# A fused attention and expert kernel on one core: the last stage moved into the main block, the expert tables made in three steps

## What is computed

```python
x = L0_attn_x                                   # 8 batches x 512 tokens x 256
x = x + _layernorm(_L0_attn_ref(_layernorm(x), ...))
x = x + _layernorm(_L0_ffn_ref(_layernorm(x), w_router, w1, b1, w2, b2))
# _L0_attn_ref: token attention with 16 heads, then channel attention with 8 heads
# _L0_ffn_ref, 8 experts, hidden width 1024, two experts per token:
probs = softmax(xf @ w_router); topk_w, topk_idx = top_k(probs, 2)
weights = sum(topk_w[..., None] * one_hot(topk_idx), axis=1)
h = gelu(einsum('te,ieh->tih', xf, w1) + b1)
out = sum((einsum('tih,ihe->tie', h, w2) + b2) * weights[..., None], axis=1)
```

## Time and profile before

| | us |
|---|---|
| runs of before, median (lowest to highest of 3) | 1127.04 (1125.57 to 1129.49) |
| the profiled execution | 1118.23 |
| its span, first to last instruction | 1116.4 |
| TensorE busy | 1032.4 (92%) |
| VectorE busy | 671.4 (60%) |
| ScalarE busy | 721.1 (65%) |
| GpSimd busy | 384.5 (34%) |
| mean granted TensorE clock | 0.975 |

### The profile page before, as it was taken

How to read it: one execution, slowest core, us unless ns; L and a number is a source line. 1 busy time by engine, 2 the same in 40 slices (tenths; PEclk the granted TensorE clock), 3 DMA queues, 4 the chain that set the end, 5 groups by cost and what they waited for, 6 DMA issues and landing times. The chain is left out here.

```text
span 1116.4 us, 17406 instructions
## 1 busy us (share of the span) xinstructions
PE 1032.4 (92%) x5756; PEld 702.8 (63%) x5756; DVE 671.4 (60%) x1902; ACT 721.1 (65%) x1106; POOL 384.5 (34%) x353
## 2 busy tenths in 40 slices
PE   5899999999999999998899996999999999989966
PEld 3234545555455455544588875888888888878842
DVE  5225265454735645354785777677677776679927
ACT  2797767667776766666655662676677766768804
POOL 5121030513323141224426243444433443254315
PEclk9899999999999999999999987999999999989989
DMA  7673816427082542832433133334443344446456
GB/s 267 133 246 61 264 31 204 122 84 256 18 261 73 174 150 69 275 148 91 147 100 115 62 135 123 124 133 148 147 161 119 138 143 142 151 143 224 149 215 256
DMA packets 48960, 167.47 MB, mean 150 GB/s; under 512 B 10160, under 2 KB 16688, under 8 KB 42864
## 3 DMA queue, kind: packets, MB, share of 16 engines
q1 hardware_dynamic: 38170, 136.94, 36.9%
q0 software_dynamic: 10560, 29.14, 8.2%
q10 hardware_dynamic: 150, 0.41, 0.2%
HBM read 102.74 MB, written 63.70 MB: 149 GB/s over the span
## 5 line engine op out<-in xcount | busy, mean ns | idle before, releaser
L589 ACT ACTIVATE E<-PS,VV 128x1024 f32<-128x1024 f32 x256 | 271.6, 1119 | 73.7 <-PE PS L974 72.6
L1737 PE MATMUL PH<-XP,W1P 128*128 128x512 f32 (+1 forms) x1104 | 233.1, 369 | 4.9 <-DVE HP L1678 4.5
L1737 PEld LDWEIGHTS PH<-XP,W1P 128*128 128x128 f32 x1104 | 185.8, 192 | 44.5 <-DVE HP L1678 8.1
L974 PE MATMUL PS<-OPB,OPA 102*128 102x512 bf16 x512 | 137.9, 386 | 11.4 <-DMA OPB<-norm_parts 5.7
L1678 DVE TENSOR_TENSOR HP<-PH,HP 128x512 fp32r<-128x512 f32 x156 | 106.7, 686 | 64.8 <-ACT HP L1584 64.3
L957 PE MATMUL PO<-E,VA 128*32 128x512 f32 x1024 | 143.5, 610 | 0.0
L1579 ACT ACTIVATE PH<-PH,B 128x512 f32<-128x512 f32 (+1 forms) x184 | 107.5, 596 | 53.9 <-PE PH L1737 44.9
L1502 POOL DMA_INDIRECT choice_rows<-Y,DI x78 | 79.3, 1016 | 182.3 <-DVE Y L1635 160.8
L974 PEld LDWEIGHTS PS<-OPB,OPA 102*128 102x128 bf16 x512 | 37.7, 98 | 155.4 <-ACT E L589 68.7
L1570 ACT CAST W2P<-WG 128x512 fp32r<-128x512 f32 x92 | 56.9, 621 | 103.6 <-PE PB L1768 63.6
L462 POOL DMA_INDIRECT expert_rows<-PAY,SLOT x64 | 62.7, 979 | 157.5 <-issue 80.1
(11 more groups left out here) (254 smaller groups left out, 1611.2 us busy)
## 6 DMA issues: line engine op xcount, KB each, us to landing
expert_rows<-ZERO SPq DMA_DIRECT2D x8, 4160.0 KB, 12.8
WG<-experts SPq DMA_DIRECT2D x23, 1152.0 KB, 5.1
WG<-experts SPq DMA_DIRECT2D x23, 1028.0 KB, 5.2
OPB<-q_parts SPq DMA_DIRECT2D x192, 64.0 KB
YC<-choice_rows SPq DMA_DIRECT2D x8, 1024.0 KB, 13.0
q_parts<-QP SPq DMA_DIRECT2D x48, 128.0 KB
OPA<-q_parts SPq DMA_DIRECT2D x31, 192.0 KB
X<-x SPq DMA_DIRECT2D x8, 512.0 KB, 11.1
```

Source lines behind the costliest of these rows:

```text
L589: a.activation(E[:, s % 2, h, :, :], PS[:, u % 2, :, :], ACT.Exp, scale=vec("tau_t")[:, 4 * (s // 2) + h:4 * (s // 2) + h + 1]).then_inc(e ...
L974: ins = t.matmul(PS[:, u % 2, jc, :], OPA[0:KA, m, key:key + P], OPB[0:KA, m, hh * N:hh * N + N], start=True, stop=True)
L1737: last = m.matmul(PH[:, u % BANKS, at:at + w], W1P[:, a, k * HID + c * P:k * HID + c * P + P], XP[:, o, k, 0:w], start=(k == 0 and (a, o) ...
```

## The change

The tables are made in three steps. `fill_begun` runs a second time, for the pairs 5 and 6 that the counts of batches 0 to 6 fix, in four sections at slots 18 to 21; BEGUN becomes 7, so units 5 and 6 are no longer joined. `fill_tables` makes the rest (25 subtiles where it were 29) in nine sections at slots 73 to 81. Both are generators that yield between sections. The steps of batch 7 behind `x2t` stand further apart. GpSimd gathers every unit at its usual place. The last stage's instructions follow the units' in the same block; SP waits for the last sends itself; the 16 warm-up matmuls are gone. Its work is cut into ten pieces: TensorE sums eight, GpSimd two (3 and 6, a batch each), roots are taken in six groups, GpSimd adds X for five pieces and VectorE for five; the sums of the last batch go to PB.

```diff
-BEGUN = -(-(2 * N * (B - 2) - NE * (2 * SUB - 1)) // (2 * SUB))
+KNOWN = [-(-(2 * N * b - NE * (2 * SUB - 1)) // (2 * SUB)) for b in (B - 2, B - 1)]
+BEGUN = KNOWN[-1]
...
-           17: [('prefix', B - 2)], 18: [('x2t', B - 1)], 20: [('qkc', B - 1)], 22: [('gram', B - 1)], 24: [('dist', B - 1)],
-           25: [('soft_c', B - 1)], 27: [('weights_c', B - 1)], 29: [('mix', B - 1)], 31: [('weff', B - 1)], 33: [('chan', B - 1)],
-           36: [('chan_add', B - 1)], 37: [('chan_stats', B - 1)], 39: [('chan_norm', B - 1)], 42: [('z3t0', B - 1)],
-           43: [('z3t1', B - 1)], 44: [('logits', B - 1)], 45: [('soft', B - 1)], 46: [('top', B - 1)], 50: [('prefix', B - 1)],
-           52: [('tables', B - 1)]}
+           17: [('prefix', B - 2)], 18: [('begin', B - 2), ('x2t', B - 1)], 19: [('begin', B - 2)], 20: [('begin', B - 2)], 21: [('begin', B - 2)], 22: [('qkc', B - 1)], 25: [('gram', B - 1)],
+           28: [('dist', B - 1)], 30: [('soft_c', B - 1)], 33: [('weights_c', B - 1)], 36: [('mix', B - 1)], 39: [('weff', B - 1)],
+           42: [('chan', B - 1)], 46: [('chan_add', B - 1)], 49: [('chan_stats', B - 1)], 53: [('chan_norm', B - 1)],
+           57: [('z3t0', B - 1)], 59: [('z3t1', B - 1)], 61: [('logits', B - 1)], 63: [('soft', B - 1)], 65: [('top', B - 1)],
+           71: [('prefix', B - 1)], **{k: [('tables', B - 1)] for k in range(73, 82)}}
...
+            known = [fill_begun(nc, dve, table_links, begun_ready, COUNT, const, QR[:, :, :].rearrange("p k n -> p (k n)"), TAKEN, tables, 0),
+                     fill_begun(nc, dve, table_links, begun_ready, COUNT, const, OT[:, :, :].rearrange("p g n -> p (g n)"), TAKEN, tables, 1)]
+            others = fill_tables(nc, dve, table_links, tables_ready, COUNT, TAKEN, const,
+                                 OT[:, :, :].rearrange("p g n -> p (g n)"), tables)
             def begin(b, par):
                 if isinstance(b, int) and b == B - 3:
-                    fill_begun(nc, dve, table_links, begun_ready, COUNT, const, QR[:, :, :].rearrange("p k n -> p (k n)"), TAKEN, tables)
+                    for _ in known[0]:
+                        pass
+                if isinstance(b, int) and b == B - 2:
+                    next(known[1], None)
             do["begin"] = begin
 
             def rest(b, par):
-                fill_tables(nc, dve, table_links, tables_ready, COUNT, TAKEN, const,
-                            OT[:, :, :].rearrange("p g n -> p (g n)"), tables)
+                next(others, None)
             do["tables"] = rest
             return do
 
...
-            experts = stage2(nc, make(apart), tables, tables_ready, const, rows, ys, experts1, experts2, begun, PB)
+            inner = ExitStack()
+            y_sent, y_rows, experts = stage2(nc, make(inner), tables, tables_ready, const, rows, ys, experts1, experts2, begun, PB)
+            inner.close()
+            last = stage3(nc, make(apart), X, const, HALF[:, :, :].rearrange("p a c -> p (a c)"), PB, ys, out, y_sent, y_rows)
             block = apart.enter_context(nc.Block())
...
             @block.vector
             def _(dve):
...
                 units()
+                last.vector(dve)
...
-        stage3(nc, make, X, const, ys, out)
...
     rows_of, most = COUNT[:, 0, :], STEPS_E // 2 - 1
...
     link(v.reduce_sum(full, over, AX.X))
+    if stage:
+        link(v.tensor_tensor(full, full, TAKEN[:, :], ALU.subtract))
+        link(v.tensor_tensor(ahead[:, 0:NE - 1], TAKEN[:, 1:NE], TAKEN[:, 0:NE - 1], ALU.subtract))
+        link(v.memset(ahead[:, NE - 1:NE], 0.0))
+        link(v.tensor_tensor(ahead, full, ahead, ALU.subtract))
+    yield
...
     for i in range(3):
+        yield
         link(v.tensor_tensor(picked, held, steps[:, i, :].unsqueeze(1).to_broadcast([P, S, VE]), ALU.mult))
         link(v.reduce_sum(chosen[:, i, :], picked, AX.X))
...
         for t in range(NUNITS):
+            if t == KNOWN[0]:
+                sp.wait_ge(begun["begun_ready"], 2)
...
-                        if t + 2 < NUNITS and t + 2 != BEGUN:
+                        if t + 2 < NUNITS:
                             gather_rows(t + 2)
                     at_slot(k)
-                    if k == REST_AT:
-                        gather_rows(BEGUN)
                 for c in range(HC):
                     k = first_slot(t) + groups_of(t) + c
                     if c == HC - 2 and t + 1 < NUNITS:
                         weigh_bias(t + 1)
                     at_slot(k)
-                    if k == REST_AT:
-                        gather_rows(BEGUN)
             send(NUNITS - 1)
-            for r in range(2):
-                pool.wait_ge(y_sent[r], 16 * turn_blocks(NUNITS - 1 - (NUNITS - 1 - r) % 2))
         return units
...
+    PIECES = [(0, 0, 2), (0, 2, 2)] + [(b, 0, C) for b in range(1, B - 1)] + [(B - 1, 0, 2), (B - 1, 2, 2)]
+    BY_PE, BY_POOL = (0, 1, 2, 4, 5, 7, 8, 9), (3, 6)
+    ROOTS = [(0, 1), (2,), (3, 4), (5,), (6, 7), (8, 9)]
+    POOL_ADDS = (0, 1, 2, 3, 6)
+    STORE_ORDER = (0, 1, 2, 4, 5, 3, 7, 6, 8, 9)
...
+    def total(i):
+        b, c, n = PIECES[i]
+        if i in BY_POOL:
+            return YC[:, b, 0, c:c + n, :]
+        if b == B - 1:
+            return PB[:, c // 2, :].rearrange("p (c e) -> p c e", c=2)
+        return S[:, BY_PE.index(i) % SLOTS, 0:n, :]
...
+    def sync(sp):
+        for r in range(2):
+            sp.wait_ge(y_sent[r], y_rows[r])
+        for i, (b, c, n) in enumerate(PIECES):
+            sp.dma_start(YC[:, b, :, c:c + n, :], yv[b][:, :, c:c + n, :]).then_inc(loaded[i], 16)
+        for i in STORE_ORDER:
+            b, c, n = PIECES[i]
+            sp.wait_ge(added[i], 1)
+            sp.dma_start(ov[b][:, c:c + n, :], T[:, b, c:c + n, :]).then_inc(stored, 16)
...
+    def tensor(pe):
+        m = nc.tensor
+        for at, i in enumerate(BY_PE):
+            b, c, n = PIECES[i]
+            pe.wait_ge(loaded[i], 16)
+            if at >= SLOTS and b < B - 1:
+                pe.wait_ge(normed, rows_before(BY_PE[at - SLOTS] + 1))
+            for a in range(0, n, 2):
+                for k in range(2):
+                    last = m.matmul(total(i)[:, a:a + 2, :].rearrange("p c e -> p (c e)"), const("ident"),
+                                    YC[:, b, k, c + a:c + a + 2, :].rearrange("p c e -> p (c e)"), start=(k == 0), stop=(k == 1))
+            last.then_inc(summed[i], 1)
...
+        def add_up(i):
+            b, c, n = PIECES[i]
+            pool.wait_ge(loaded[i], 16)
+            g.tensor_tensor(YC[:, b, 0, c:c + n, :], YC[:, b, 0, c:c + n, :], YC[:, b, 1, c:c + n, :], ALU.add).then_inc(summed[i], 1)
+        def root(k):
+            at = columns(ROOTS[k][0], ROOTS[k][-1])
+            pool.wait_ge(var_ready, 2 * (k + 1))
+            g.tensor_tensor(R[:, 2, at], R[:, 0, at], half[:, 0:at.stop - at.start], ALU.pow).then_inc(roots, 1)
+            pool.wait_ge(roots, k + 1)
+            g.tensor_tensor(R[:, 3, at], R[:, 1, at], R[:, 2, at], ALU.mult).then_inc(scaled, 1)
+        root(0)
+        add_up(3)
+        add(0)
+        root(1)
+        add(1)
+        add_up(6)
+        root(2)
+        add(2)
+        root(3)
+        root(4)
+        add(3)
+        root(5)
+        add(6)
...
+        for k, group in enumerate(ROOTS):
+            for i in group:
+                b, c, n = PIECES[i]
+                dve.wait_ge(summed[i], 1)
+                for a in range(n):
+                    link(v.bn_stats(ST[:, columns(i).start + a, :], total(i)[:, a, :]))
+            dve.wait_ge(links, at[0])
+            cols = columns(group[0], group[-1])
+            for a in range(cols.start, cols.stop):
+                link(v.bn_aggr(MV[:, a, :], ST[:, a, :]))
+            dve.wait_ge(links, at[0])
+            v.tensor_scalar_add(R[:, 0, cols], MV[:, cols, 1], EPS).then_inc(var_ready, 1)
+            v.tensor_scalar_mul(R[:, 1, cols], MV[:, cols, 0], -1.0).then_inc(var_ready, 1)
+            if k >= LAG:
+                for i in ROOTS[k - LAG]:
+                    if i not in POOL_ADDS:
+                        add(i)
+        for k in range(len(ROOTS) - LAG, len(ROOTS)):
+            for i in ROOTS[k]:
+                if i not in POOL_ADDS:
+                    add(i)
```

197 lines of the change are left out of this document (88 added, 109 removed).

## The result

| | before | changed | ratio |
|---|---|---|---|
| first comparison, median us (lowest to highest) | 1126.3 (1123.9 to 1129.5) | 1138.3 (1135.4 to 1140.3) | 1.0094 [1.0058, 1.0130] |
| the same kernel once more, below | 1119.5 | 1118.6 | 0.9982 [0.9958, 1.0007] |
| profiled execution (span) | 1118.2 (1116.4) | 1137.5 (1135.7) | |

Slower by 0.94%, where 0.7% faster was forecast (1119.5 against 1127.0). A comparison is a set of kernels measured side by side with the kernel before. Both rows of ratios are needed: what the change costs depends on pauses of TensorE that come in some comparisons and not in others, and the profile of before that I read was taken without them.

The account below looks back on a forecast made before the run. TensorE was taken as the bound, VectorE close behind. Tail -1.6 and last stage -6.0 gave -7.6 us: 1110.6 profiled, 1119.5 with the 8.8 us to the median of 1127.0 kept; range 1110 to 1128.

Parts of the forecast that it names:

- 8.8 above it: Whole kernel: the median exceeds the profiled execution's 1118.2 us by 8.8, and the changed kernel's would by the same.
- the one for XP 1.4: End of unit 4's second half: TensorE done at 12.4 us, then waiting 1.4 us for VectorE's second XP.
- delays VectorE, not TensorE: Unit 4: prefix, 2.2 us of VectorE behind group 7, costs TensorE nothing.
- 2 x 0.3: Units 5 and 6, no longer joined: 0.3 us more each, 0.6 us together.
- 20.6: Units 0 to 5: TensorE's idle time in us after the change, 1.8 more than the 18.8 before.
- sections 8 and 9: Tables in unit 5's first half: section 8 behind group 0 costs 0.6 us, section 9 behind group 1 costs 1.7.
- my bounds of 12 and 30: Units 0 to 5: the prediction is wrong if TensorE's idle time is under 12 or over 30 us.
- -1.6: Whole tail: 1.8 us more idle, 4 less from the slow clock, 0.6 more un-joined, together -1.6 us.
- -6.0: Last stage: earlier issue and smaller first piece, with 1.4 us added for GpSimd's collisions, end at 1110.4, -6.0 us.
- rival 1: Last stage: GpSimd becomes the bound by the SBUF lock with VectorE; total -4.6 us, 1122.4, or -0.2; chance 0.15.
- Rival 2: Slots 64 to 82: VectorE's backlog lands on TensorE in full; total +9 us, 1136, at half 1128; chance 0.13.

Follow-up runs that it names:

- e7: The units of before with the new last stage, TensorE summing all ten pieces, VectorE making all additions, GpSimd only roots: ratio 1.0052 to the kernel before.
- e8: The units of before with the new last stage, GpSimd making roots and two sums, VectorE all additions: ratio 0.9954 to the kernel before.
- e4: The changed kernel with units 5 and 6 joined again: ratio 1.0063 to the kernel before.
- e13: The changed kernel unaltered, measured once more: ratio 0.9982 to the kernel before, which took 1119.5 us.
- e10: The kernel before with 7 more indirect DMAs on GpSimd in unit 4, making a row of 15: ratio 1.0064.
- e11: As e8, with 40 warm-up matmuls on TensorE before the first load lands: ratio 0.9969 to the kernel before.
- e16: The kernel before with 7 more indirect DMAs on GpSimd in unit 4, a second time: ratio 1.0053.
- e17: The kernel before with 7 more indirect DMAs on GpSimd in unit 4, a third time: ratio 1.0080.
- e14: The changed kernel with its block closed without GpSimd's DRAIN, run beside e13: ratio 0.9966 to the kernel before.
- e2: The units of before with the new last stage in the same block: ratio 0.9972 to the kernel before.
- e3: The changed kernel with prefix of the last batch at slot 67 instead of 71: ratio 0.9999 to the kernel before.

## Why the prediction was wrong

- **"the median of the runs is 1127.0, 8.8 above it, and I put the same difference there"** is the step that failed first. The 8.8 us was not a constant. The profiled execution had no pause under "issue" in a chunk. The units of before do have them where before takes 1128 or 1134: e7, with these units, shows 13.3 us in unit 4's second half, where the earlier trace rows has 12.0, and 22.4 in unit 1's, where that profile has 16.1 (e8: 13.2 and 24.3). The changed kernel meets this with 32 more matmuls in two halves and a row of 16 indirect DMAs, and took 19.7 us more, not 8.8.
- **Unit 4's second half.** I counted "the one for XP 1.4" and treated GpSimd's prefix scatter as free ("delays VectorE, not TensorE"). Without the pauses that was right: 13.8 us measured. With them it is 26.5. I named every VectorE step that moved, but not what the scatter's new place made on GpSimd: directly behind send and gather instead of alone.
- **Units 5 and 6 un-joined, "2 x 0.3"**: 12.0 each without the pauses, as said; 13.3 and 13.1 with them, 2.9 us more in all (e4).
- **The tail's stalls, "20.6"** of idle time in units 0 to 5. In e13, length less TensorE's busy time over its six stretches, 16.9: 5.4 in units 0 and 1 (forecast 5.8), 0.6 in unit 2 (1.1), 1.0 in unit 3 (1.0), 3.2 in unit 4's first half (3.5), and for the tables 1.57 + 5.08 = 6.7 (9.2: sections 8 and 9 cost nothing, I had given them 2.3). So idle time fell from 18.8 by 1.9, where I had it rise by 1.8. TensorE's busy time in the six stretches fell from 180.9 to 178.5, 2.4, where the clock and unit 5's un-joined half should give 3.7. In the first comparison TensorE's idle time is 28.4, inside my bounds of 12 and 30, for a cause that wasn't in the list. Without the pauses units 0 to 6 take 219.0 us; the old units took 223.0, 222.6, 222.0, 220.5 and 220.0 in before, e10, e11, e16 and e17. The tail gives about -3 us; I had -1.6.
- **The last stage, "-6.0".** Issue 5.9 us after the last expert matmul instead of 8.0 (2.1, right); TensorE's end 34.4 (34.5, right). The chain behind it is 13.1 us in e14 and not 10.8. Part of that is terms that I sized wrong: GpSimd's additions took 2.35 and the halves 1.27 where nothing blocked them (priced at 1.89, from an addition with other inputs, and 1.04), a root of eight columns 1.65 (priced at 1.04). The rest is rival 1's mechanism: held by VectorE, two roots of the first profile took 2.54 and 1.92, and held by GpSimd, VectorE's `tensor_scalar` up to 2.3. In all -3.9 instead of -6.0. Then **GpSimd's DRAIN**, +5.0, which no step had: I removed the block's price and did not ask what of it comes back at the only block's end. Together +1.1 in e13, +2.0 in the first profile.
- **Sum.** Without pauses -3 + 1.1 = -2 us, measured 0.9982, within what can be told from no change. With them, units 0 to 6 take 234.0 instead of 219.0: 12.8 the stall, 2.3 the two un-joined halves, 2.2 in unit 3, less 2.8 because VectorE catches up during the stall, the rest small. The old units take 225.8 in e2, 3.8 more than without (230.7 and 231.1 in e7 and e8, where before took 1134). So the change should lose 15.0 - 3.8 = 11.2 us against before; the two ratios are 0.0112 apart, 12.6 us.
- **Rival 2** named unit 4 and slots 64 to 82 and a time of 1136 us, near the result, but for another reason: VectorE's steps never cost their full length. It was right by place, not by mechanism. Its chance of 0.13 came from counting VectorE alone. (Its 18.5 us of VectorE's steps are 19.1 by its own rows: 2.75, 2.2 and 14.1.)

What stays open: what in the chip makes the pauses, why they differ between comparisons (each on its own chip), and what sets the DRAIN at 1.1 to 1.7 us or at 9.2. The old units never ran with the long row where the pauses come: e10, e16 and e17 met none. e3 has the same 220 indirect DMAs as the changed kernel in another order, and a short DRAIN.

## What to carry to other kernels

When a change moves a step, write down for each queue what will then stand in an unbroken row, DMA issues above all; a step is not free because the busy engines don't see it. When the profiled execution is faster than the medians by more than a measurement's error, the profile may lack something that the medians pay, and a change can make more of it: don't carry the difference over as a constant. And before a block is merged into another, list what its end does on each engine (here a DRAIN behind 220 indirect DMAs), since that comes back at the next end: put it where its engine idles.
